# Local rounds of a fused kernel: two steps of VectorE's order moved, four copies given from GpSimd to ScalarE

## What is computed

```
def step(S, inp):                            # delta rule, per token
    S = S * exp(g)
    dv = (v - k.S) * b
    S = S + outer(k, dv);  o = q.S

def _layer(x, ...):                          # local attention, twice
    h = shift_token(x)                       # upper 64 features one token late
    q, k, v = split(h @ wqkv)
    q, k = l2norm(q) * qs, l2norm(k) * ksc
    q, k = rotary_xpos(q, k)
    x = x + local_attention(q, k, v) @ wo    # windows of 64, own and previous
    h = layer_norm(shift_token(x))
    a, g = split(h @ w1 + b1)
    return x + (a * gelu(g)) @ w2 + b2
```

## Time and profile before

| | us |
|---|---|
| median of 3 runs | 2034.4 (2033.83 to 2039.69) |
| profiled execution, its own time | 2048.09 |
| its span | 2046.3 |
| mean granted clock of TensorE in it | 0.89 of full speed |

### The profile page before, as it was taken

One profiled execution on the slowest core, in us unless ns is written; L12 is line 12 of the kernel. 1 busy time (PEld: TensorE's weight loads), 2 busy tenths in 40 slices (PEclk: granted clock), 3 DMA queues, 4 the chain that ended last, 5 costly groups with the idle time before them and its releaser, 6 DMA issues. The chain is left out here.

```text
span 2046.3 us, 31347 instructions
## 1 busy us (share of the span) xinstructions
PE 1549.5 (76%) x10312; PEld 1086.4 (53%) x10376; DVE 1517.5 (74%) x2701; ACT 1129.3 (55%) x3167; POOL 1301.7 (64%) x1780
## 2 busy tenths in 40 slices
PE   6989898888998748731578777777778777777765
PEld 4667677677776643311355555555555555555543
DVE  2466759677686863995688888888888888888843
ACT  2356566665666733331356666666666666666643
POOL 0455446365555710554888888888888888888700
PEclk9889889998999878965689999999999999999877
DMA  2555565564756814763000000000000000000004
GB/s 84 180 179 205 172 216 193 180 207 166 244 170 207 281 50 128 234 178 112 1 15 3 17 17 17 17 6 12 17 17 17 16 6 12 17 17 17 4 3 123
DMA packets 137573, 191.97 MB, mean 94 GB/s; under 512 B 65730, under 2 KB 94788, under 8 KB 137284
## 3 DMA queue, kind: packets, MB, share of 16 engines
q0 software_dynamic: 36864, 134.76, 19.5%
q1 hardware_dynamic: 95314, 50.98, 9.1%
q10 hardware_dynamic: 5234, 4.23, 0.7%
HBM read 166.22 MB, written 23.72 MB: 93 GB/s over the span
## 5 line engine op out<-in xcount | busy, mean ns | idle before, releaser
L304 POOL DMA_INDIRECT l_rows<-in_table,l_idx x256 | 333.9, 1304 | 294.5 <-DVE l_idx L635 179.4
L437 PE MATMUL l_acc<-l_rows,ident 128*128 128x128 f32 x2048 | 310.4, 307 | 73.9 <-ACT l_rows L531 67.5
L437 PEld LDWEIGHTS l_acc<-l_rows,ident 128*128 128x128 f32 x2048 | 275.8, 214 | 109.1 <-ACT l_rows L531 100.7
L531 ACT ACTIVATE l_rows<-l_rows,l_act 128x128 f32<-128x128 f32 x1024 | 306.1, 387 | 2.1
L1315 ACT ACTIVATE lo_prob<-lo_s_ps,lo_nmx,lo_rn 128x128 f32<-128x128 f32 x512 | 226.7, 460 | 43.5 <-DVE lo_nmx L1579 41.7
L1467 POOL TENSOR_TENSOR lo_c<-lo_c 128x1024 f32<-128x1024 f32 x64 | 150.8, 2356 | 11.2 <-DVE lo_c L1569 6.8
L585 DVE TENSOR_TENSOR l_rows<-l_rows,xn_tok 128x2048 f32<-128x2048 f32 x64 | 145.9, 2279 | 8.5 <-DMA l_rows<-in_table,l_idx 8.5
L586 DVE TENSOR_REDUCE l_dot<-l_rows 128x16 f32<-128x2048 f32 x64 | 146.3, 2286 | 2.2
L403 PE MATMUL l_S<-top_out,l_AT 128*128 128x144 f32 (+3 forms) x832 | 126.4, 301 | 21.6 <-ACT l_AT L522 17.2
L522 ACT ACTIVATE l_AT<-l_log,top_bias 128x512 f32<-128x512 f32 (+1 forms) x96 | 63.9, 684 | 133.4 <-PE l_log L395 118.6
L403 PEld LDWEIGHTS l_S<-top_out,l_AT 128*128 128x128 f32 (+2 forms) x832 | 112.2, 202 | 34.5 <-ACT l_AT L522 22.6
(11 more groups left out here) (266 smaller groups left out, 3972.4 us busy)
## 6 DMA issues: line engine op xcount, KB each, us to landing
scratch_ops<-pr_ops SPq DMA_DIRECT2D x4, 1568.0 KB, 5.7
lo_de_ops<-scratch_ops SPq DMA_DIRECT2D x16, 392.0 KB, 3.7
l_rows<-in_table,l_idx POOLq DMA_INDIRECT x256
lo_de_qo<-scratch_qo SPq DMA_DIRECT2D x16, 256.0 KB, 3.9
x_tok<-in_x SPq DMA_DIRECT2D x8, 256.0 KB, 5.2
scratch_q<-pr_stage_q SPq DMA_DIRECT2D x8, 256.0 KB, 3.8
scratch_k<-pr_stage_k SPq DMA_DIRECT2D x8, 256.0 KB, 2.3
pr_Yq<-scratch_q SPq DMA_DIRECT2D x8, 256.0 KB, 3.0
```

Of the source, the lines that this page charges most:

```text
L304: pool.indirect_dma_start(rows[L][:, r % SLOTS, p, :], None, a[f"table{L}"], bass.IndirectOffsetOnAxis(ap=at[:, p:p + 1], axis=0)).then_in ...
L437: ins = pe.matmul(out, m["ident"][:], rows[L][:, r % SLOTS, p, (FAN + f) * D:(FAN + f + 1) * D], start=False, stop=(L == 5 and k == PICK - ...
L531: ins = act.activation(z, z, ACT.Copy, scale=actv[L][:, r % 2, k:k + 1])
```

## The change

VectorE: `residual(w)` goes ahead of `normalise(v, 0)`; `query` and `o_normalise` go behind `normed(w)`; `gate` 0 and 1 go ahead of `answer`, which is cut in two, its first reduction ahead of `gate` 2 and the rest behind it. `maxima` makes both reductions, then one product for both, and `mx_ready` counts two a unit instead of four.

ScalarE instead of GpSimd makes `split_v(u)`, behind the second copy of V, and `shift(u + 1)`, behind `square_c(w)`; `shift(0)` is ahead of the rounds. GpSimd keeps `rotate` alone.

PE: the fourth turned probability block goes to `o_ps` and no longer to `ft_ps`, `turn_out` goes to `ft_ps` and no longer to `h_ps` and stands behind the turned probabilities; waits are changed to match. ScalarE's `keep_out` follows it.

```diff
@@ -1055,7 +1055,7 @@
         f2_full, f2_kept = st("qk_turned", 4), st("qk_kept", 4)
-        s_full, mx_ready, prob_ready, pn_ready = st("s_full", 2), st("mx_ready", 4), st("prob_ready", 4), st("pn_ready", 2)
+        s_full, mx_ready, prob_ready, pn_ready = st("s_full", 2), st("mx_ready", 2), st("prob_ready", 4), st("pn_ready", 2)
         pt_full, pt_kept, pv_full, o_kept = st("pt_full", 4), st("pt_kept", 4), st("pv_full", 2), st("o_kept", 2)
@@ -1063,8 +1063,8 @@
         S_ready, qS_read, o_ready, oss_ready, orms_ready, o_normed = (st("de_" + k) for k in ("S_ready", "qS_read", "o_ready", "oss_ready", "orms_ready", "o_normed"))
-        olog_ready = st("de_olog_ready")
-        turn_bank = lambda kind, k: o_ps if (kind, k) == ("qk", 2) else h_ps if (kind, k) == ("prob", 2) else ft_ps
+        olog_ready, o_summed = st("de_olog_ready"), st("de_o_summed")
+        turn_bank = lambda kind, k: o_ps if (kind, k) == ("qk", 2) or (kind, k) == ("prob", 3) else h_ps if (kind, k) == ("prob", 2) else ft_ps
         NH_ = NB // HB
@@ -1157,20 +1157,18 @@
                     pe.wait_ge(f2_kept.sem, f2_kept.after(v))
-                    if v:
-                        pe.wait_ge(pt_kept.sem, pt_kept.after(v - 1))
+                    if v - 2 >= B:
+                        pe.wait_ge(t_kept.sem, t_kept.after(v - 2 - B))
                 elif (j, e) == (0, 1):
...
                         pe.wait_ge(y2_ready.sem, y2_ready.after(v - 1))
-                    if v > B:
-                        pe.wait_ge(t_kept.sem, t_kept.after(v - 1 - B))
                 else:
                     if v + 1 < U:
-                        pe.wait_ge(f2_kept.sem, f2_kept.after(v + 1))
-                    elif v:
-                        pe.wait_ge(u_ready.sem, u_ready.after(v - 1))
+                        pe.wait_ge(f2_kept.sem, f2_kept.after(v + 1, 3))
+                    else:
+                        pe.wait_ge(o_kept.sem, o_kept.after(v, 1))
                 for k in range(NP):
@@ -1183,8 +1181,6 @@
                     pe.wait_ge(o_kept.sem, 2 * v + j)
-                if j and v + 1 < U:
-                    pe.wait_ge(f2_kept.sem, f2_kept.after(v + 1, 3))
                 for k in range(NP):
@@ -1201,8 +1197,6 @@
                     pe.wait_ge(y2_ready.sem, y2_ready.after(w - 1))
-                if w > B:
-                    pe.wait_ge(t_kept.sem, t_kept.after(w - 1 - B))
                 for k in range(NP):
@@ -1226,7 +1220,10 @@
                 else:
-                    pe.wait_ge(pt_kept.sem, pt_kept.after(min(w + 1, U - 1), 2 if w + 1 < U else 4))
+                    if w + 1 < U:
+                        pe.wait_ge(pt_kept.sem, pt_kept.after(w + 1, 2))
+                    else:
+                        pe.wait_ge(t_kept.sem, t_kept.after(w - 1 - B))
                 dst = (h_ps, v_ps, ft_ps)[k]
@@ -1240,8 +1237,10 @@
                 pe.wait_ge(y2_ready.sem, y2_ready.after(x))
+                if x + 2 < U:
+                    pe.wait_ge(f2_kept.sem, f2_kept.after(x + 2))
                 for i in (0, 1):
-                    ins = pe.transpose(h_ps[:, i * P:(i + 1) * P], y2[:, i * P:(i + 1) * P], m["ident"][:])
+                    ins = pe.transpose(ft_ps[:, i * P:(i + 1) * P], y2[:, i * P:(i + 1) * P], m["ident"][:])
                 ins.then_inc(t_full.sem, 1)
@@ -1258,11 +1257,12 @@
                     turn_qk(v, 1, 1)
+                if lw:
+                    turn_prob(w, 1, 0)
+                    turn_prob(w, 1, 1)
                 if lx and x >= B:
...
                 if lw:
-                    turn_prob(w, 1, 0)
-                    turn_prob(w, 1, 1)
                     weigh(w, 1)
@@ -1307,7 +1307,7 @@
                 for e in (0, 1):
-                    act.wait_ge(mx_ready.sem, mx_ready.after(v, 2 * j + e + 1))
+                    act.wait_ge(mx_ready.sem, mx_ready.after(v, j + 1))
                     if v:
@@ -1360,6 +1360,22 @@
+            def shift(u):
+                if u >= B:
+                    act.wait_ge(y2_ready.sem, y2_ready.after(u - B))
+                if u >= 2:
+                    act.wait_ge(v_full.sem, v_full.after(u - 2))
+                src = yin(u)
+                act.copy(hT[0:64, u % 2, :], src[0:64, :])
+                act.copy(hT[64:P, u % 2, 1:T], src[64:P, 0:T - 1]).then_inc(hT_ready.sem, 1)
+            def split_v(u):
+                act.wait_ge(v_kept.sem, v_kept.after(u))
+                if u >= 2:
+                    act.wait_ge(pv_full.sem, pv_full.after(u - 2))
+                act.copy(VE[0:64, u % 2, :], V[0:64, u % 3, 1, :])
+                act.copy(VE[64:P, u % 2, :], V[64:P, u % 3, 0, :]).then_inc(ve_ready.sem, 1)
             def o_roots(h):
@@ -1370,8 +1386,10 @@
                 act.wait_ge(t_full.sem, t_full.after(x - B))
-                act.copy(sized(m["xn_tok"][:, (x - B) * 2:(x - B) * 2 + 2, :]), h_ps[:, 0:T]).then_inc(t_kept.sem, 1)
-
+                act.copy(sized(m["xn_tok"][:, (x - B) * 2:(x - B) * 2 + 2, :]), ft_ps[:, 0:T]).then_inc(t_kept.sem, 1)
+            act.wait_ge(consts.sem, 1)
+            shift(0)
             for t in range(U + 3):
@@ -1383,19 +1401,23 @@
                     keep_v(u, 0)
+                if lw:
+                    keep_pT(w, 1, 0)
+                    keep_pT(w, 1, 1)
                 if lx and x >= B:
...
                 if lw:
-                    keep_pT(w, 1, 0)
-                    keep_pT(w, 1, 1)
                     keep_o(w, 1)
...
                     keep_v(u, 1)
+                    split_v(u)
                 if lw:
                     square_c(w)
+                if u + 1 < U:
+                    shift(u + 1)
                 if lv:
@@ -1414,7 +1436,7 @@
         def _(pool):
-            ch, chs = Chain(ctx, nc, pool, "lo_pool", 3), Chain(ctx, nc, pool, "lo_pool_shift", 1)
+            ch, chs = Chain(ctx, nc, pool, "lo_pool", 2), None
             chd = Chain(ctx, nc, pool, "de_pool", 0)
@@ -1422,17 +1444,6 @@
             pool.wait_ge(consts.sem, 1)
-
-            def shift(u):
-                if u >= B:
-                    pool.wait_ge(y2_ready.sem, y2_ready.after(u - B))
-                if u >= 2:
-                    pool.wait_ge(v_full.sem, v_full.after(u - 2))
-                src = yin(u)
-                chs.begin(u)
-                chs.link(pool.tensor_copy(hT[0:64, u % 2, :], src[0:64, :]))
-                pool.tensor_copy(hT[64:P, u % 2, 1:T], src[64:P, 0:T - 1]).then_inc(hT_ready.sem, 1)
-                pool.wait_ge(hT_ready.sem, hT_ready.after(u))
@@ -1473,22 +1484,8 @@
-            def split_v(u):
-                ch.unit, ch.n = u, 2
-                pool.wait_ge(v_kept.sem, v_kept.after(u))
-                if u >= 2:
-                    pool.wait_ge(pv_full.sem, pv_full.after(u - 2))
-                ch.link(pool.tensor_copy(VE[0:64, u % 2, :], V[0:64, u % 3, 1, :]))
-                ch.end()
-                pool.tensor_copy(VE[64:P, u % 2, :], V[64:P, u % 3, 0, :]).then_inc(ve_ready.sem, 1)
-                pool.wait_ge(ve_ready.sem, ve_ready.after(u))
-
-            shift(0)
             for u in range(U):
-                if u + 1 < U:
-                    shift(u + 1)
                 rotate(u)
-                split_v(u)
@@ -1508,10 +1505,13 @@
-            def answer(h):
+            def answer(h, part):
                 p, n0 = h // 2 % 2, HB * (h % 2)
                 o = o_[:, h % 2]
-                chd.link(dve.tensor_reduce(o.rearrange("p i n x -> p (i n x)"), qS[:].rearrange("p i (a k) -> p (i a) k", k=HD), AX.X, ALU.add))
+                if part == 0:
+                    dve.tensor_reduce(o.rearrange("p i n x -> p (i n x)"), qS[:].rearrange("p i (a k) -> p (i a) k", k=HD), AX.X, ALU.add).then_inc(o_summed.sem, 1)
+                    return
+                dve.wait_ge(o_summed.sem, o_summed.after(h))
                 dve.tensor_tensor(o, o, qo[:, p, 1, :, n0:n0 + HB, :], ALU.add).then_inc(o_ready.sem, 1)
@@ -1572,11 +1572,12 @@
                 dve.wait_ge(rn_ready.sem, rn_ready.after(v))
+                if v:
+                    dve.wait_ge(prob_ready.sem, prob_ready.after(v - 1, 2 * j + 2))
                 for e in (0, 1):
-                    if v:
-                        dve.wait_ge(prob_ready.sem, prob_ready.after(v - 1, 2 * j + e + 1))
-                    chm.link(dve.tensor_reduce(nmx[:, j, e, :], s_ps[e][:].rearrange("p (k t) -> p k t", t=P), AX.X, ALU.max, negate=True))
-                    dve.tensor_tensor(nmx[:, j, e, :], nmx[:, j, e, :], rn[:, v % 2, j, e:HEADS:2], ALU.mult).then_inc(mx_ready.sem, 1)
+                    ins = dve.tensor_reduce(nmx[:, j, e, :], s_ps[e][:].rearrange("p (k t) -> p k t", t=P), AX.X, ALU.max, negate=True)
+                chm.link(ins)
+                dve.tensor_tensor(nmx[:, j], nmx[:, j], rn[:, v % 2, j, 0:HEADS].rearrange("p (k e) -> p e k", e=2), ALU.mult).then_inc(mx_ready.sem, 1)
@@ -1632,29 +1633,32 @@
                     sums_of(u, 0)
+                if lw:
+                    residual(w)
```

(21 more changed lines are left out.)

## The result

The changed kernel takes 2057.5 us in the median where the kernel before, on the same chips, takes 2037.1: a ratio of 1.0109 (95% interval 1.0074 to 1.0145), slower by 20 us. A second set of runs on one chip gave 2056.8 against 2039.5, 1.0082 (1.0066 to 1.0098). The forecast was 2032, within 6 us of no change; the kernel became slower, and its time lies inside the range given.

The account below looks back on a forecast made before the run. The prediction took a loop of hand-overs between engines, no single engine, to bound the kernel. Rounds of 16.1 + 14.7 = 30.8 us against 30.75 and a shorter end gave -2 together; with the runs' lower median, 2032 us, range 1992 to 2064.

Parts of the forecast that it names:

- the chain: Local phase: a loop of hand-overs between the engines, from floors round to floors, ties together each round of 30.75 us.
- P: Mark in each round: VectorE's end of the first rotation parts, where the maxima follow; P to F was 13.17 us.
- Part 2: Four copies on ScalarE: 1.5 us a round, with bounds of 1.1 and 2.5.
- the third rival: ScalarE's chain from exponentials to root, with four copies, decides; at 2.5 us of copies 32 us slower, 2064; chance 0.26.
- Part 5: Stretch F to P: last reduction of the answer at F + 6.35, P at F + 16.1 where it was 18.23.
- F: Mark in each round: start of VectorE's floors; F to P was 18.23 us.
- The sum: Whole round: 16.1 + 14.7 = 30.8 us against 30.75; +1.6 us over 32 rounds, -2 to -4 at the end.
- 0.47: Chance given to the forecast of 2032 itself: of that faster 0.20, same 0.17, slower 0.10.
- The meeting: At P the maxima's product waits out GpSimd's addition; the rival that it is missed: 1.1 us a round, 1999, chance 0.20.
- GpSimd as the bound: Rival: GpSimd bounds the round, so its 2.27 us a round come off whole, 73 us, 1961; chance 0.07.
- ScalarE's chain: The third rival: ScalarE's work from exponentials to root, with four copies in it, decides; 2064 at its upper bound; chance 0.26.

Follow-up runs that it names:

- 1: The changed kernel with the four copies back on GpSimd, all else as changed: 2047.9 us, 1.0050 of the kernel before.
- 4: The changed kernel with query and o_normalise again ahead of residual and normalise(v, 0): 2024.2 us, 0.9930 of the kernel before.
- 5: The changed kernel with GpSimd's c1 addition made to wait for VectorE's product of the maxima: 2036.6 us, 0.9982 of the kernel before.
- 8: The changed kernel with o_roots behind the exponentials of w's second half on ScalarE, no longer ahead: 2028.7 us, 0.9934 of the kernel before.
- 6: The changed kernel with two reductions and two products for the maxima, as in the kernel before: 2065.5 us, 1.0130 of the kernel before.
- 7: The changed kernel with all three gates behind the whole answer again: 2063.4 us, 1.0106 of the kernel before.
- 2: The kernel before with only the four copies moved to ScalarE: 2059.0 us, 1.0092 of the kernel before.
- 3: The changed kernel with all four copies on ScalarE late, behind keep_pT(v, 0, 1): 2056.4 us, 1.0079 of the kernel before.
- all four edits: The changed kernel with query and o_normalise ahead, copies late, GpSimd's addition behind the maxima and o_roots behind the exponentials: 1929.7 us, 0.9463 of the kernel before.

## Why the prediction was wrong

- **What bounds it, and the shape of the chain: right.** Every new wait stands at its place: the residual's matmuls 1.02 us (1.1 said), prob 1.17 (1.0) and 1.8 (2.1), gate 0 0.61 (0.6), hn 1.56 (0.9); GpSimd began its addition 0.2 behind P. Four edits at those places moved the time by 8 to 30 us (1, 4, 5 and 8), and two of which the chain let expect little hardly did (6, and 7 by 5 us).
- **Part 2 failed, in its size.** I took 1.5 us for the four copies, with the overlap of neighbouring activations. They took 1.27 (1254.89 to 1256.16) and 0.85 (1256.57 to 1257.42), 2.12: each lasts 0.61 or 0.41 and the next starts only behind it, while the squares and the copy of V ahead of them last 0.62 and start 0.48 apart. By the Trainium skill (VectorE: DVE Perf Modes, the section on the errata for instructions that read SBUF) a ScalarE instruction from SBUF to SBUF takes 224 cycles and one per element at 1.2 GHz, from which I estimate 613 and 400 ns. The trace agrees, with 0.62 and 0.41. Two of each are 2.03 by that estimate, and it is what I should have taken. The step then worked as the third rival said, excess in full: hn at P + 11.87 instead of 11.15, 0.60 of it by the copies. The query cost 0.38 less than its 1.92, since GpSimd stood still beside it (o_normalise 0.38 us, 0.68 before): floors at P + 15.05 instead of 14.7.
- **Part 5 was short by 0.3 to 0.4.** 16.39 in the best rounds instead of 16.1, in small pieces (the last reduction at F + 6.45 instead of 6.35, the reciprocal at F + 10.92 instead of 10.7, second k kept after a wait of 0.30), and 16.52 in the mean, because one round in four has 16.8 to 17.1, each with a granted clock near 0.5 in the 2 us behind F, where PE makes Gelu's input. I took the clock for a cost that the change removes; it moved to other stretches.
- **The sum.** The middle rounds are 0.35 + 0.42 = 0.77 us over their 30.8. Over all rounds it is 31.30 - 30.8 = 0.5, 16 us in 31. What I had added for the ends came: 2 us at the head (the first residual 73 us into the phase instead of 75) and 3 at the tail (15.0 instead of 18.2). So the local phase, forecast at some 1045 (1046.8 less 2), is 1058.6, and 14 of the 25 us between 2032 and 2057.5 are in it. Another 8 come from the trace that I read, which was that much longer than the second one in the same phase (a round of 30.75 against 30.59, a tail of 18.2 against 15.2). The last 3 or 4 lie outside the phase or in the spread of the runs; no run separates them. A forecast of zero as the difference of two sums, 30.8 and 30.75, each right to 0.4 us at best, deserved less trust than its 0.47; the slower side was the better bet, as in this kernel the copies' bounds of 1.1 and 2.5 lay 0.4 below and 1.0 above what I took.
- **The rivals.** The meeting was not missed in the changed kernel, and 5 shows what missing it gives: 17 us of local phase, not 35. (Its 1999 is 35 off the 2034 shown, without the 2 us of the end; 35 off the forecast is 1997.) GpSimd as the bound is refuted by 1 and 2. ScalarE's chain is what happened, with 2.12 us where the rival had 2.5.
- **Which part of the change costs.** The query behind hn, 30 us (4); the copies in the chain, 8 us here and 20 alone (1, 2). Gates ahead give 5 at most; one product for the maxima nothing. These do not add up to the 20 us of the whole: without the query's move the change is 14 us faster than before, and the copies alone cost as much as everything together. The residual's place and PE's banks and turns were not tried by themselves, so what they give is not shown.

## What to carry to other kernels

Where queues of several engines hand work round in a ring, walk the ring with the trace's durations: a step moved off a busy engine gains nothing if that engine is the one that waits, and a step moved out of a wait into the ring costs its full length. Look for instructions on the ring that something else put there by issue order alone (a root that nobody needs yet ahead of exponentials that all wait for): moving three such steps and adding one wait was worth 126 us, where balancing the loads with the other moves lost 20. And judge a single edit by the halves of the round, not by the total: 3 looked like nothing and was 0.9 us a round, spent at once on a slower PE.

## What was unexpected

- A change of the order on other engines moves the stretches of low granted clock. Copies late left PE's idle time in the middle rounds at 177 us, and even raised the mean granted clock of these rounds from 0.90 to 0.94, but the low stretch now fell where VectorE waits for PE: the same 32 score matmuls took 1.10 us in one round and 1.99 in another with the granted clock at 1.00 and 0.50. With all four edits the mean is 0.97, and they gave 126 us together against 75 singly.
- An added wait made the kernel faster: GpSimd's addition of 2.35 us held back by some 1.4 us let a 128x8 product take 0.17 us instead of 1.28, with 17 us less in the whole.
- The copies on 64 partitions and SBUF on both sides took 0.61 us for 512 columns and 0.41 for 256 on ScalarE, against 0.60 for 512 columns on GpSimd: no faster per copy, only elsewhere.
